# A second PSUM bank for the A3 product of a LoRA pair in a dense mixture of experts on eight cores

## The chip, the cores and the metric

The kernel runs on the 8 cores of one Trainium2 chip, two dies of four cores. Every core works on one batch element of 2048 tokens by 1024 features and has its own copy of all weights; the cores exchange nothing. The time is that of the slowest core, in microseconds (us) of the device. The engines are called PE (TensorE matmuls), PEld (TensorE weight loads), DVE (VectorE), ACT (ScalarE), POOL (GpSimd) and SP (SyncE).

## What is computed

One transformer layer: a conditionally routed attention, then a feed-forward part in which all 8 experts run on all tokens and are mixed by gates (two gates per token are not zero). The change lies in the second part. Cut to what matters:

```python
def _lora_in(xf, W, b, A, B):
    base = einsum('td,ehd->teh', xf, W)
    low = einsum('ter,ehr->teh', einsum('td,erd->ter', xf, A), B)   # r = 16
    return base + low + b
h1 = _lora_in(xf, W1, b1, A1, B1)
h3 = _lora_in(xf, W3, b3, A3, B3)
g = silu(h1) * h3
y_e = _lora_out(g, W2, b2, A2, B2)
y = einsum('te,ted->td', gates, y_e)
```

Here xf is the layer-normed input (2048 tokens per core, 1024 features), the hidden size is 2048, and the rank of A and B is 16.

## The kernel before

The kernel is written with a queue of instructions for each engine. `P.do(engine, emit, waits, inc)` appends an instruction (or a chain of matmuls) to the queue of one engine; `waits` are pairs of a semaphore and the count that it must have reached, read when the code is written, and `inc` is the semaphore that the last instruction of the entry raises. `flush` writes the queues out and leaves out a wait that the same engine has already made for the same or a higher count. Each engine works through its queue in the order written, so a wait holds back all that is behind it. `drain=True` makes the engine's next instruction wait for this one to be complete.

The stages "a" to "f" hold layer norms, routing, both attentions and the gates; they fill the first 3495 us. Stage "g", the rest, is the feed-forward part. Its outer loop `for eq_i in range(32)` runs over 8 experts (e) times 4 quarters of the hidden size (q). Weights of the next step are fetched by POOL's DMA queue into the other of two buffers (`wdma`); the small `a1te`, `a3te`, `b2te`, `b1ce`, `b3ce` have one buffer and are fetched once per expert, when the expert before has been finished. Inside it, `for tc in range(4)` runs over four blocks of 512 tokens. One pass of this inner loop puts on PE, in this order:

- only with q = 0: `mku(a1te)`, 8 matmuls that accumulate A1 times x into PSUM tile `pMISC[0:16, 0:512]` (line 1413), which DVE copies to `u1sb` (line 1426); then `mku(a3te)`, 8 matmuls of A3 times x into the same `pMISC[0:16, 0:512]`, which DVE copies to `u3sb` (line 1431). The second chain waits for the first copy. So the u products of an expert are made once for each token block, 32 times in the whole kernel.
- the gate row spread over 128 partitions, one matmul into `pch(3)` (line 1435), copied by DVE to `gateb` (line 1441).
- four times (hc), 8 + 1 matmuls for h1 into bank 0 or 2 of `pSIM` and 8 + 1 for h3 into bank 1 or 3 (lines 1452 and 1457; the ninth adds the LoRA part from `u1sb` or `u3sb`). ACT takes h1 out with Silu into `gtmp1` (line 1467) and h3 with a bias into `gtmp2` (line 1476), and DVE forms gTq from them and the gate (lines 1481 and 1487).
- 8 chains of 4 matmuls for y (line 1526; with q = 3 a fifth, line 1532, and for the first expert a sixth, line 1537), each added by DVE to `x1` (line 1549).
- `emit_u2`, 4 matmuls into `pMISC[32:48]` (line 1494), added by DVE to `u2sb` (line 1505); with q = 3 this comes ahead of the y chains.

PSUM here: `pSIM` has 2048 float32 columns per partition, four banks of 512 that `pch(0)` to `pch(3)` name; `pMISC` has one such bank. `S["mm"]` and `S["sim"]` are raised by PE, `S["vec"]`, `S["vec2"]`, `S["vec3"]`, `S["tev"]` and `S["oe"]` by DVE, `S["scl"]` and `S["scl2"]` by ACT.

Of the kernel before, what the change touches and what calls it, by code (L numbers as in the profile page):

```python
# [189 lines left out]
def build(debug_taps=()):  # L190
# [164 lines left out]
    a1te = sat("a1te", [128, 128], BF16, WS + 6400)  # L355
    a3te = sat("a3te", [128, 128], BF16, WS + 6656)
# [10 lines left out]
    pSIM = nc.alloc_psum_tensor("pSIM", [128, 2048], F32)  # L367
    pT = nc.alloc_psum_tensor("pT", [128, 2048], BF16)
    pOUT = nc.alloc_psum_tensor("pOUT", [128, 128], F32)
    pMISC = nc.alloc_psum_tensor("pMISC", [128, 512], F32)  # L370
# [10 lines left out]
    S = {k: Sem(nc, k) for k in names}  # L381
    nc.const_aps.register(F32, 1e-5, fconst[0:1, 0:1])
    P = Prog(nc, S)
# [30 lines left out]
    for _e in ("tensor", "vector", "scalar", "gpsimd"):  # L414
        P.do(_e, lambda E: E.nop(),
             waits=[(S["sdc"], SD_CONST), (S["sgc"], S["sgc"].n)])
# [41 lines left out]
    for dc in range(8):  # L458
# [3 lines left out]
             waits=ld + [(S["mm"], S["mm"].n)], inc=S["scl"], drain=True)  # L462
        def mk(d=dc):
            def f(E):
# [12 lines left out]
             inc=S["mm"])  # L477
# [5 lines left out]
    for dc in range(8):  # L483
# [3 lines left out]
             waits=ld + [(S["scl"], S["scl"].n),  # L487
                         (S["mm"], max(0, S["mm"].n - 1))],
             inc=S["vec"], drain=True)
        P.do("vector", (lambda d=dc: lambda E:  # L490
                        E.tensor_mul(xlch(d)[:, :], xlch(d)[:, :], rB[:, :]))(),
             inc=S["vec"], drain=True)
        P.do("scalar", (lambda d=dc: lambda E:
                        E.activation(xsq[:, :], xlch(d)[:, :], AF.Square))(),
             waits=[(S["vec"], S["vec"].n), (S["mm"], S["mm"].n)],
             inc=S["scl"], drain=True)
        def mk(d=dc):
# [19 lines left out]
         waits=[(S["mm"], S["mm"].n)], inc=S["vec"], drain=True)  # L517
    P.do("vector", lambda E: E.tensor_scalar_mul(c0_row, pSIM[0:1, 0:2048], 1 / 1024.0),
         inc=S["vec"], drain=True)
    P.do("vector", lambda E: E.tensor_copy(sr_row, pSIM[32:33, 0:2048]),  # L520
         inc=S["vec"], drain=True)
    P.do("vector", lambda E: E.tensor_mul(c1_row, c0_row, c0_row),
         inc=S["vec"], drain=True)
# [4 lines left out]
         waits=[(S["vec"], S["vec"].n)], inc=S["scl"], drain=True)  # L528
    P.do("scalar", lambda E: E.activation(sr_row, sr_row, AF.Sqrt),
         inc=S["scl"], drain=True)  # L530
    P.do("vector", lambda E: E.reciprocal(c1_row, t_row),
         waits=[(S["scl"], S["scl"].n)], inc=S["vec"], drain=True)
    P.do("vector", lambda E: E.tensor_scalar_max(sr_row, sr_row, 1e-12),
         inc=S["vec"], drain=True)
    P.do("vector", lambda E: E.reciprocal(sr_row, sr_row), inc=S["vec"], drain=True)
    P.do("vector", lambda E: E.tensor_scalar_mul(sr_row, sr_row, 32.0),
         inc=S["vec"], drain=True)
    P.do("vector", lambda E: E.tensor_mul(c0_row, c0_row, c1_row),
         inc=S["vec"], drain=True)
    P.do("vector", lambda E: E.tensor_scalar_mul(c0_row, c0_row, -1.0),  # L540
         inc=S["vec"], drain=True)
# [3 lines left out]
    if "route_s" in debug_taps:  # L545
# [5 lines left out]
         waits=[(S["vec"], S["vec"].n)], inc=S["c1p"], drain=True)  # L551
    cur_eps = 4.0
    logk = math.log(1152.0)
    for it in range(20):
        inv = 1.0 / cur_eps
        P.do("gpsimd", lambda E: E.tensor_sub(u_rt, s_rt, rl_rt),
             waits=[(S["c1s"], S["c1s"].n), (S["c1p"], S["c1p"].n)],
             inc=S["c1p"], drain=True)
        P.do("vector", lambda E: E.reduce_max(sc_rt[:, 0:1], u_rt, axis=AX.X),
             waits=[(S["c1p"], S["c1p"].n)], inc=S["c1v"], drain=True)  # L560
# [3 lines left out]
             inc=S["c1v"], drain=True)  # L564
# [3 lines left out]
             waits=[(S["c1v"], S["c1v"].n)], inc=S["c1s"], drain=True)  # L568
        P.do("vector", lambda E: E.reduce_sum(sc_rt[:, 2:3], rl_rt, axis=AX.X),
             waits=[(S["c1s"], S["c1s"].n)], inc=S["c1v"], drain=True)  # L570
        P.do("scalar", lambda E: E.activation(sc_rt[:, 3:4], sc_rt[:, 2:3], AF.Ln),
             waits=[(S["c1v"], S["c1v"].n)], inc=S["c1s"], drain=True)
        P.do("gpsimd", lambda E: E.tensor_sub(sc_rt[:, 4:5], sc_rt[:, 3:4],
                                              sc_rt[:, 1:2]),
             waits=[(S["c1s"], S["c1s"].n)], inc=S["c1p"], drain=True)
# [3 lines left out]
             inc=S["c1p"], drain=True)  # L579
        P.do("scalar", lambda E: E.activation(rl_rt, s_rt, AF.Relu,  # L580
                                              bias=sc_rt[:, 5:6], scale=1.0),
             waits=[(S["c1p"], S["c1p"].n)], inc=S["c1s"], drain=True)
# [5 lines left out]
    for dc in range(8):  # L588
# [3 lines left out]
             waits=ld + [(S["scl"], S["scl"].n)], inc=S["vec"], drain=True)  # L592
        P.do("vector", lambda E: E.tensor_mul(xlt[:, :], xlt[:, :], rB[:, :]),
             inc=S["vec"], drain=True)
        P.do("vector", lambda E: E.tensor_mul(xlt[:, :], xlt[:, :], c1B[:, :]),
             inc=S["vec"], drain=True)
        P.do("vector", lambda E: E.tensor_add(xlt[:, :], xlt[:, :], c0B[:, :]),
             inc=S["vec"], drain=True)
# [4 lines left out]
             inc=S["vec"], drain=True)  # L603
    P.flush("p2b")
    if "ln2T" in debug_taps:
# [4 lines left out]
          inc=S["sgw"])  # L610
# [788 lines left out]
    for eq_i in range(32):  # L1399
# [4 lines left out]
        if q == 0:  # L1404
            P.do("vector", lambda E: E.memset(u2sb, 0.0),
                 waits=[(S["mm2"], S["mm2"].n)], inc=S["vec3"], drain=True)
        for tc in range(4):
            if q == 0:
                def mku(att, tc=tc):
                    def f(E):  # L1410
                        ins = None
                        for dc in range(8):
                            ins = E.matmul(pMISC[0:16, 0:512],  # L1413
                                           att[:, 16 * dc:16 * dc + 16],
                                           xl2T[:, 2048 * dc + 512 * tc:
                                                2048 * dc + 512 * tc + 512],
                                           start=(dc == 0), stop=(dc == 7))
                        return ins
                    return f
                P.do("tensor", mku(a1te),  # L1420
                     waits=[sg_at[eq_i], (S["scl2"], S["scl2"].n),
                            (S["vec3"], S["vec3"].n), (S["vec"], S["vec"].n),
                            (S["sim"], S["sim"].n)],
                     inc=S["mm"])
                P.do("vector", (lambda tc=tc: lambda E:
                                E.tensor_copy(u1sb[:, 512 * tc:512 * tc + 512],
                                              pMISC[0:16, 0:512]))(),
                     waits=[(S["mm"], S["mm"].n)], inc=S["vec"], drain=True)
                P.do("tensor", mku(a3te), waits=[(S["vec"], S["vec"].n)], inc=S["mm"])
                P.do("vector", (lambda tc=tc: lambda E:  # L1430
                                E.tensor_copy(u3sb[:, 512 * tc:512 * tc + 512],  # L1431
                                              pMISC[0:16, 0:512]))(),
                     waits=[(S["mm"], S["mm"].n)], inc=S["vec"], drain=True)
            P.do("tensor", (lambda e=e, tc=tc: lambda E:
                            E.matmul(pch(3), sel8[:, 128 * e:128 * e + 128],  # L1435
                                     gatesF[:, 512 * tc:512 * tc + 512],
# [161 lines left out]
```

How the kernel before makes its waits and increments, by code:

```python
                    def body(E):  # L169
                        seen = {}
                        prev_pend = [None]
                        for (waits, emit, inch, k, pend) in ops:
                            allw = list(waits)
                            if prev_pend[0] is not None:
                                allw.append(prev_pend[0])
                            for (s, n) in allw:
                                h = s.h
                                if seen.get(id(h), -1) < n:
                                    E.wait_ge(h, n)
                                    seen[id(h)] = n
                            ins = emit(E)
                            if inch is not None:
                                ins.then_inc(inch, k)
                            prev_pend[0] = (pend[0], pend[1]) if pend else None
```

## Time and profile before

| what | us |
|---|---|
| median of 2 timed runs | 7972.79 |
| the two runs | 7962.31 and 7983.27 |
| the profiled execution, its own time | 7924.43 |
| span of its slowest core (core 1) | 7922.9 |
| spans of its eight cores | 7885.8 to 7922.9 |

The profiled execution is one run of the same program, recorded by the hardware. Its span goes from the first to the last instruction of one core, and its own time adds what lies around that (1.5 us). Durations are read from this execution, which is 48.4 us, or 0.6%, below the median of the timed runs. "Busy" sums the time in which an engine worked; "granted clock" is the share of TensorE's full 2.4 GHz that was granted in a stretch, 0.50 being the lower of the two levels, 1.2 GHz.

### The profile page before, as it was taken

To read this page: it belongs to the slowest core of one execution; us is meant where nothing else is said; L and a number is where in the kernel's file an instruction comes from. 1 tells how busy PE (TensorE), PEld (TensorE's weight loads), DVE (VectorE), ACT (ScalarE), POOL (GpSimd) and SP (SyncE) were. 2 spreads that over 40 slices of the span, in tenths; PEclk is the share of its full clock that TensorE was granted. 3 is DMA by queue.
4 is the path that set the end of the run, shared out by engine and by line. 5 is a ranking of instruction groups with operands and counts; after the bars stand their busy time and mean duration, and the time that the engine had idled before them with its cause. 6 is when DMAs were issued, how large, how long until landed. Compare 5 with 4: busy or idle time off the path is not lost.

```text
span 7922.9 us, 72055 instructions; the slowest of 8 cores (7885.8 to 7922.9 us)
## 1 busy us (share of the span) xinstructions
PE 5513.9 (70%) x22384; PEld 2099.6 (27%) x22384; DVE 3300.1 (42%) x6024; ACT 1412.4 (18%) x1824; POOL 305.9 (4%) x337
## 2 busy tenths in 40 slices
PE   5141133247687776238888889889888888898897
PEld 1020000113454452013223323223233233232232
DVE  2755444476666662443323333333233233333332
ACT  1012100002343341011111111111111111111111
POOL 0012100000000000000000000000000000000000
PEclk8575555566555557569879989999899899898998
DMA  2110000020000001021211112121212112121211
GB/s 94 52 11 0 0 0 0 6 48 6 1 1 1 1 1 53 1 33 17 33 17 20 30 17 33 17 33 17 33 17 33 17 17 33 17 33 17 33 17 43
DMA packets 149719, 169.26 MB, mean 21 GB/s; under 512 B 56132, under 2 KB 125268, under 8 KB 142948
## 3 DMA queue, kind: packets, MB, share of 16 engines
q0 software_dynamic: 140688, 111.63, 9.5%
q1 hardware_dynamic: 8660, 53.04, 1.9%
q8 instruction: 191, 3.13, 0.2%
q14 instruction: 180, 1.47, 0.1%
HBM read 267.68 MB, written 8.39 MB: 35 GB/s over the span
## 4 chain that ended last, share of the span: by engine, by line
PE 47%; DVE 5%; issue 3%; ACT 1%; DMA 1%; POOL 0%; DVEq 0%; ACTq 0%; PEldq 0%; POOLq 0%
PE pSIM L1452 24%; PE pSIM L1526 13%; PE pSIM L1457 4%; DVE x L1549 2%; PE pMISC L1413 2%; PE pMISC L1494 2%; PE pSIM L1532 1%; ACT gtmp L1476 1%; DVE gTq L1487 1%; DVE gtmp L1481 1%; DMA b3ce<-b3c 1%; DVE u2sb L1505 0%; PE pSIM L1435 0%; DVEq L179 0%; DVE u3sb L1431 0%
## 5 line engine op out<-in xcount | busy, mean ns | idle before, releaser
L1526 PE MATMUL pSIM<-gTq,w2b 128*128 128x512 bf16 x4096 | 1203.7, 441 | 310.3 <-DVE gTq L1487 225.5
L1549 DVE SCALAR_TENSOR_TENSOR x<-pSIM,x 128x512 f32<-128x512 f32 x1024 | 708.3, 692 | 780.4 <-PE pSIM L1526 445.8
L1452 PE MATMUL pSIM<-xl2T,w1b 128*128 128x512 bf16 x4096 | 997.5, 387 | 21.1 <-DVE u3sb L1431 21.1
L1481 DVE TENSOR_TENSOR gtmp<-gtmp,gtmp 128x512 bf16<-128x512 bf16 x512 | 217.7, 425 | 1870.9 <-ACT gtmp L1476 1870.9
L1452 PE MATMUL pSIM<-xl2T,w3b 128*128 128x512 bf16 x4096 | 972.9, 380 | 0.0
L1467 ACT ACTIVATE gtmp<-pSIM,b1ce 128x512 bf16<-128x512 f32 x512 | 352.8, 689 | 2950.3 <-PE pSIM L1457 2923.8
L1526 PEld LDWEIGHTS pSIM<-gTq,w2b 128*128 128x128 bf16 x4096 | 385.0, 108 | 1051.1 <-issue 862.7
L1452 PEld LDWEIGHTS pSIM<-xl2T,w1b 128*128 128x128 bf16 x4096 | 363.7, 99 | 517.6 <-issue 165.6
L1452 PEld LDWEIGHTS pSIM<-xl2T,w3b 128*128 128x128 bf16 x4096 | 358.6, 98 | 481.2 <-issue 118.4
L824 PE MATMUL pT<-idbf,lattnT 128*128 128x128 bf16 x128 | 33.9, 265 | 648.5 <-DVE lattnT L819 648.5
L1476 ACT ACTIVATE gtmp<-pSIM,b3ce 128x512 bf16<-128x512 f32 x512 | 352.6, 689 | 716.2 <-PE pSIM L1457 716.2
L1025 DVE TENSOR_REDUCE smwk<-pSIM 128x1 f32<-128x512 f32 x512 | 354.1, 692 | 59.6 <-PE pSIM L1006 6.2
L1072 PE MATMUL pOUT<-attnT,hv 128*65 128x128 bf16 x2048 | 265.8, 309 | 39.4 <-DVE attnT L1102 25.9
L1006 PE MATMUL pSIM<-hk,hq 64*128 64x512 bf16 x512 | 240.4, 620 | 10.7 <-ACT attnbf L1045 5.3
L1487 DVE TENSOR_TENSOR gTq<-gtmp,gateb 128x512 bf16<-128x512 bf16 x512 | 217.7, 425 | 55.8 <-DVE gtmp L1481 3.2
L1063 PE MATMUL pT<-idbf,attnbf 128*128 128x128 bf16 x2048 | 240.6, 312 | 0.0
L1072 PEld LDWEIGHTS pOUT<-attnT,hv 128*65 128x65 bf16 x2048 | 210.3, 169 | 84.4 <-issue 68.8
L1063 PEld LDWEIGHTS pT<-idbf,attnbf 128*128 128x128 bf16 x2048 | 206.9, 145 | 52.5 <-issue 52.3
L1057 ACT COPY attnT<-pT 128x1024 bf16<-128x1024 bf16 x128 | 129.6, 1013 | 506.0 <-PE pT L1063 506.0
L1457 PE MATMUL pSIM<-u1sb,b1tqb 16*128 16x512 bf16 x512 | 199.6, 390 | 0.0
L1129 PE MATMUL pMISC<-denrow,ones_f 1*128 1x256 f32 x128 | 76.0, 695 | 175.4 <-DVE denrow L1124 132.9
L1494 PE MATMUL pMISC<-gTq,a2tqb 128*16 128x512 bf16 x512 | 150.5, 422 | 68.3 <-DVE gTq L1487 68.3
(265 smaller groups left out, 4779.5 us busy)
## 6 DMA issues: line engine op xcount, KB each, us to landing
w1b<-w1q POOLq DMA_DIRECT2D x32, 1024.0 KB, 9.6
w3b<-w3q POOLq DMA_DIRECT2D x32, 1024.0 KB, 13.7
w2b<-w2q POOLq DMA_DIRECT2D x32, 1024.0 KB, 16.8
xs<-xT SPq DMA_DIRECT2D x24, 1024.0 KB, 4.8
xc<-xT SPq DMA_DIRECT2D x16, 1024.0 KB, 4.9
out<-x SPq DMA_DIRECT2D x8, 1024.0 KB, 10.2
wst<-wqkv POOLq DMA_DIRECT2D x8, 256.0 KB, 5.1
cos<-cos SPq DMA_DIRECT2D x1, 1024.0 KB
```

What stands on the lines that cost most here:

```text
L1025: E.reduce_max(smwk[:, 2 + kc:3 + kc], pSIM[:, 512 * kc:512 * kc + 512], axis=AX.X))(),
L1063: ins = E.transpose(pT[:, 1024 * half + 128 * (j - j0): 1024 * half + 128 * (j - j0) + 128], attnbf[:, 128 * j:128 * j + 128], idbf[:, :])
L1072: ins = E.matmul(pOUT[0:65, 0:128], hv[:, 520 * j + 65 * h:520 * j + 65 * h + 65], attnT[:, 128 * j:128 * j + 128], start=(start and j == ...
L1452: E.matmul(pSIM[:, 512 * bank:512 * bank + 512], wb[:, 512 * dc + 128 * hc:512 * dc + 128 * hc + 128], xl2T[:, 2048 * dc + 512 * tc: 2048 ...
L1457: return E.matmul(pSIM[:, 512 * bank:512 * bank + 512], btq[:, 128 * hc:128 * hc + 128], usb[:, 512 * tc:512 * tc + 512], start=False, sto ...
L1467: E.activation(gtmp1[:, :], pSIM[:, 512 * b:512 * b + 512], AF.Silu, bias=b1ce[:, hcg:hcg + 1], scale=1.0))(),
L1476: E.activation(gtmp2[:, :], pSIM[:, 512 * b:512 * b + 512], AF.Identity, bias=b3ce[:, hcg:hcg + 1], scale=1.0))(),
L1481: P.do("vector", lambda E: E.tensor_mul(gtmp1[:, :], gtmp1[:, :], gtmp2[:, :]), waits=[(S["scl"], S["scl"].n), (S["scl2"], S["scl2"].n), ( ...
L1487: E.tensor_mul(gTq[:, 512 * hc:512 * hc + 512], gtmp1[:, :], gateb[:, :]))(),
L1494: ins = E.matmul(pMISC[32:48, 0:512], a2tqb[par][:, 16 * hc:16 * hc + 16], gTq[:, 512 * hc:512 * hc + 512], start=(hc == 0), stop=(hc == 3))
L1526: ins = E.matmul(pch(yb), w2b[par][:, 1024 * hc + 128 * dc: 1024 * hc + 128 * dc + 128], gTq[:, 512 * hc:512 * hc + 512], start=(hc == 0), ...
L1549: E.scalar_tensor_tensor(x1[:, 2048 * dc + 512 * tc: 2048 * dc + 512 * tc + 512], pch(yb), 1.0, x1[:, 2048 * dc + 512 * tc: 2048 * dc + 51 ...
```

## The change

The chain for A3 now writes columns 1024 to 1535 of `pSIM`, bank 2, partitions 0 to 15, in place of `pMISC`, and DVE copies it from there. Its wait for DVE's copy of the A1 product is replaced: it waits for DVE's copy of the A3 product of the token block before (`u3ev`), and for ACT's last reads of `pSIM` (`scl`, `scl2`). The A1 chain waits for its own last copy (`u1ev`) in place of the newest count of `vec`; its other waits stay. In the first token block of an expert neither dictionary has an entry, and both chains wait for the newest count of `vec`, as before; for the A3 chain that is the copy of the A1 product.

```diff
+        if q == 0:
+            u1ev, u3ev = {}, {}
         for tc in range(4):
             if q == 0:
-                def mku(att, tc=tc):
+                def mku(att, dst, tc=tc):
                     def f(E):
                         ins = None
                         for dc in range(8):
-                            ins = E.matmul(pMISC[0:16, 0:512],
+                            ins = E.matmul(dst,
                                            att[:, 16 * dc:16 * dc + 16],
...
-                P.do("tensor", mku(a1te),
+                P.do("tensor", mku(a1te, pMISC[0:16, 0:512]),
                      waits=[sg_at[eq_i], (S["scl2"], S["scl2"].n),
-                            (S["vec3"], S["vec3"].n), (S["vec"], S["vec"].n),
+                            (S["vec3"], S["vec3"].n),
+                            (S["vec"], u1ev.get(tc - 1, S["vec"].n)),
                             (S["sim"], S["sim"].n)],
                      inc=S["mm"])
...
-                P.do("tensor", mku(a3te), waits=[(S["vec"], S["vec"].n)], inc=S["mm"])
+                u1ev[tc] = S["vec"].n
+                P.do("tensor", mku(a3te, pSIM[0:16, 1024:1536]),
+                     waits=[(S["vec"], u3ev.get(tc - 1, S["vec"].n)),
+                            (S["scl"], S["scl"].n), (S["scl2"], S["scl2"].n)],
+                     inc=S["mm"])
                 P.do("vector", (lambda tc=tc: lambda E:
                                 E.tensor_copy(u3sb[:, 512 * tc:512 * tc + 512],
-                                              pMISC[0:16, 0:512]))(),
+                                              pSIM[0:16, 1024:1536]))(),
                      waits=[(S["mm"], S["mm"].n)], inc=S["vec"], drain=True)
+                u3ev[tc] = S["vec"].n
```

No instruction is added, removed or moved on any engine; waits differ. PE's queue at the start of the second token block of an expert, with the waits that are left after `flush`, before:

```order
L1494 MATMUL pMISC<-gTq,a2tqb_155 16x512 x4
L1413 MATMUL pMISC<-xl2T,a1te 16x512 [waits vec3,sim]
L1413 MATMUL pMISC<-xl2T,a1te 16x512 x7
L1413 MATMUL pMISC<-xl2T,a3te 16x512 [waits vec]
L1413 MATMUL pMISC<-xl2T,a3te 16x512 x7
L1435 MATMUL pSIM<-gatesF,sel_56 128x512 [waits oe]
L1452 MATMUL pSIM<-xl2T,w1b_165 128x512 [waits vec]
```

The same place in PE's queue after the change (lines are numbered 2 to 8 higher there):

```order
L1502 MATMUL pMISC<-gTq,a2tqb_155 16x512 x4
L1415 MATMUL pMISC<-xl2T,a1te 16x512 [waits vec3,sim]
L1415 MATMUL pMISC<-xl2T,a1te 16x512 x7
L1415 MATMUL pSIM<-xl2T,a3te 16x512 x8
L1443 MATMUL pSIM<-gatesF,sel_56 128x512 [waits oe]
L1460 MATMUL pSIM<-xl2T,w1b_165 128x512 [waits vec]
```

The A3 chain has lost its only wait; the A1 chain keeps its waits for `vec3` and `sim`, and the first h1 matmul its wait for `vec`. This holds for token blocks 2 to 4 of each expert, 24 times. At the first token block of the kernel's first expert the queue reads, after the change:

```order
L1415 MATMUL pMISC<-xl2T,a1te 16x512 [waits sgp0,scl2,vec3,vec,sim]
L1415 MATMUL pMISC<-xl2T,a1te 16x512 x7
L1415 MATMUL pSIM<-xl2T,a3te 16x512 [waits vec,scl]
L1415 MATMUL pSIM<-xl2T,a3te 16x512 x7
L1443 MATMUL pSIM<-gatesF,sel_56 128x512 [waits tev,vec2,oe]
```

There the A3 chain still waits for `vec`, and so it does at the first block of the seven other experts.

## Rows read from the trace of the kernel before

**Rows 1.** The page: its head, and busy time by engine.
```profile
span 7922.9 us, 72055 instructions; the slowest of 8 cores (7885.8 to 7922.9 us)
PE 5513.9 (70%) x22384; PEld 2099.6 (27%) x22384; DVE 3300.1 (42%) x6024; ACT 1412.4 (18%) x1824; POOL 305.9 (4%) x337
```

**Rows 2.** Windows: stretch, busy us of PE, PEld, DVE, ACT, POOL; granted clock; DMA.
```profile
0.00:3450.00 3450.00, 1647.32 (x7632) 779.04 (x7632) 1902.15 (x3606) 701.94 (x793) 140.03 (x105) 0.57 0.06 16
3495.00:7922.00 4427.00, 3866.53 (x14752) 1320.56 (x14752) 1388.78 (x2407) 706.70 (x1025) 153.81 (x215) 0.91 0.15 25
```

**Rows 3.** Waits of PE, 3495 to 7922 us: total us, times, longest.
```profile
PE pSIM L1526 <- DVE gTq L1487: 225.5, 96, 2.7
PE pMISC L1413 <- DMA b3ce<-b3c: 129.5, 8, 88.7
...
PE pMISC L1413 <- DVE u1sb L1426: 32.0, 32, 1.0
PE pMISC L1413 <- DVE u2sb L1505: 26.7, 24, 1.1
...
PE pSIM L1452 <- DVE u3sb L1431: 21.1, 32, 0.7
```

**Rows 4.** Timeline at the first expert's fourth token block: start, duration, what.
```profile
3607.61 0.68 DVE L1505 SCALAR_TENSOR_TENSOR u2sb<-pMISC,u2sb 16x512 f32<-16x512 f32 x1 [0.27 <-PE pMISC L1494]
...
3608.54 1.89 PE L1413 MATMUL pMISC<-xl2T,a1te 128*16 128x512 bf16 x8 [1.11 <-DVE u2sb L1505]
3610.60 0.68 DVE L1426 CAST u1sb<-pMISC 16x512 bf16<-16x512 f32 x1 [2.31 <-PE pMISC L1413]
...
3611.43 1.89 PE L1413 MATMUL pMISC<-xl2T,a3te 128*16 128x512 bf16 x8 [1.00 <-DVE u1sb L1426]
...
3613.25 0.39 PE L1435 MATMUL pSIM<-gatesF,sel 8*128 8x512 bf16 x1
3613.49 0.68 DVE L1431 CAST u3sb<-pMISC 16x512 bf16<-16x512 f32 x1 [2.21 <-PE pMISC L1413]
3614.27 0.69 DVE L1441 CAST gateb<-pSIM 128x512 bf16<-128x512 f32 x1
...
3614.32 0.59 PE L1452 MATMUL pSIM<-xl2T,w1b 128*128 128x512 bf16 x2 [0.68 <-DVE u3sb L1431]
```

**Rows 5.** The chain that ended last, the second expert's second token block.
```profile
4120.50 1.90 PE pMISC L1413 x8
...
4122.57 0.69 DVE u1sb L1426
...
4123.39 1.90 PE pMISC L1413 x8
...
4125.45 0.69 DVE u3sb L1431
...
4126.28 1.89 PE pSIM L1452 x8
```

**Rows 6.** Timeline: the A3 chains of token blocks 2 to 4, first and last of 24.
```profile
3538.82 1.89 PE L1413 MATMUL pMISC<-xl2T,a3te 128*16 128x512 bf16 x8 [1.00 <-DVE u1sb L1426]
...
7473.78 1.89 PE L1413 MATMUL pMISC<-xl2T,a3te 128*16 128x512 bf16 x8 [1.00 <-DVE u1sb L1426]
```

**Rows 7.** Timeline: both chains of the fourth expert's first token block.
```profile
5171.19 3.57 PE L1413 MATMUL pMISC<-xl2T,a1te 128*16 128x512 bf16 x8 [5.97 <-DMA b3ce<-b3c]
...
5175.77 3.57 PE L1413 MATMUL pMISC<-xl2T,a3te 128*16 128x512 bf16 x8 [1.00 <-DVE u1sb L1426]
```

**Rows 8.** Windows, columns as in rows 2: 10 us of h chains; three passes.
```profile
3510.00:3520.00 10.00, 10.00 (x43) 3.66 (x42) 1.70 (x4) 3.97 (x6) 0.00 (x0) 1.00 0.01 2
5216.43:5251.86 35.43, 29.85 (x127) 10.65 (x126) 11.67 (x20) 5.51 (x8) 0.00 (x0) 1.00 0.00 0
5251.86:5289.18 37.32, 31.69 (x127) 11.23 (x126) 11.67 (x20) 5.51 (x8) 0.00 (x0) 0.95 0.00 1
6271.50:6311.60 40.10, 34.54 (x127) 11.85 (x126) 11.67 (x20) 5.51 (x8) 0.00 (x0) 0.86 0.27 46
```

**Rows 9.** Cores: two of the eight, span and mean granted clock.
```profile
core 0: 7885.8 us, clock 0.767
core 1: 7922.9 us, clock 0.763
```

## The prediction

> **What bounds the kernel now.** I read the page first, for who is busy. PE is busy for 5513.9 of 7922.9 us [rows 1]. The windows then show two unlike halves: up to 3450 us PE works 1647 us at a mean granted clock of 0.57, from 3495 us on it works 3867 of 4427 us at 0.91 [rows 2]. The second half is the expert stage, in which the change lies, and there PE is the bound: DVE has work for 1389 of the same 4427 us, less than a third. What can be won in this stage is therefore idle time of PE and time at the lower clock, and nothing in the first 3495 us is touched.
>
> The list of waits, for that stage, says where PE stands still [rows 3]. The largest is the wait of the first y chain for gTq, 225.5 us in 96 pieces. The 129.5 us for a DMA are mostly the fetch ahead of the stage (88.7 us in one piece); the other seven come to 40.8 us, 5.8 us each, at the start of an expert. The A3 chain waits for the copy of the A1 product 32 times, 32.0 us together, 1.00 us each. Two waits stand on either side of it: the A1 chain for the sum into u2sb (24 times, 26.7 us), and the first h1 chain for the copy of u3 (32 times, 21.1 us). The change can touch the middle one alone.
>
> The timeline of one such place shows it in order [rows 4]: PE starts the A1 chain at 3608.54, DVE's copy runs from 3610.60 for 0.68 us, the A3 chain starts at 3611.43. Then the gate matmul follows at 3613.25 with no gap, DVE copies u3 from 3613.49, and h1 starts at 3614.32 after 0.68 us of waiting. The chain of waits that ended last runs through this place: chain, copy, chain, copy, chain [rows 5]. So a microsecond taken out between the two chains moves everything behind it forward.
>
> **What the change removes.** In token blocks 2 to 4 of each expert, 3 x 8 = 24 times, the A3 chain has no wait left and goes behind the A1 chain at once. In the first token block of each expert it still waits for the A1 copy, so 8 of the 32 waits stay at 1.00 us. The price of one removed wait can be read as a distance between starts, which includes the end of the pipeline. From the A1 chain to the A3 chain it is 3611.43 - 3608.54 = 2.89 us. What it will be without the wait has its nearest row in the next step: from the A3 chain to the gate matmul, which follows without a wait, it is 3613.25 - 3611.43 = 1.82 us. The gain is 2.89 - 1.82 = 1.07 us a time, and 24 x 1.07 = 25.7 us. The lower end is the idle time as shown, 24 x 1.00 = 24.0 us. For the upper end the A3 chain would follow with the spacing that matmuls have inside a chain. A chain of 8 is recorded with 1.89 us and one matmul alone with 0.39 [rows 4], so seven spacings take 1.50 us, 0.214 each, and eight 1.71. The upper end is 24 x (2.89 - 1.71) = 28.3 us. I take 25.7, whose row has a chain of the same 8 matmuls in front.
>
> The Trainium skill, "TensorE: Matmul & The Clock Gate", section "Back-to-back issue gap", puts the spacing at the full clock at columns / 2.4 GHz plus about 2.5 ns, 216 ns for 512 columns. By that rule the chain would be followed after 1.73 us and the sum would be 24 x 1.16 = 27.8 us, an estimate near my upper end; the rows show 1.82 us at a change of the weights' shape, and the choice between the two is worth 2 us.
>
> All 24 places run at the full clock, as the first and the last of them show: 1.89 us for a chain of 8 [rows 6], against 3.57 us at 1.2 GHz where an expert has just waited for its DMA [rows 7]. The eight places at the lower clock are first blocks, where the wait stays. So no part of the 24 is worth more because PE is slow there.
>
> **What the change moves or adds.** DVE's copy of u1, 0.68 us, now lies beside the A3 chain of 1.89 us; it is done about 1 us before that chain ends, and DVE is idle then (it waited 2.21 us for the A3 chain [rows 4]). The cover therefore holds. What is late next is the u3 copy, 0.68 us between the A3 chain and h1, as now: the wait of 21.1 us in 32 pieces stays and is not larger. It is 0.68 us since the gate matmul covers part of the copy, and that matmul stays in its place. If DVE were late with u1 by over 1 us it would be late with u3 as well, and h1 would wait for it; nothing in rows 4 makes it late.
>
> The added waits cost nothing. PE's wait for `scl` and `scl2` asks for ACT's last reads of pSIM in the token block before; the y chains have already waited for the same counts, so in blocks 2 to 4 no wait is written. The wait for the u3 copy of the block before was passed by the h1 chains. In the first block of the kernel `scl` is asked for, 88.7 us of DMA wait [rows 3] behind ACT's last work of the stage before. The A1 chain's weaker wait for `vec` wins nothing either, since the y chains waited for a later count; what holds it is u2sb, 1.11 us [rows 4], which stays. Bank 2 is next written by the second h1 chain, over 5 us after the copy of u3 began, and h1 has waited for that copy. No DMA is moved: the weights wait for the ends of steps, each about 3 us earlier after a q = 0 step, and the DMA engines are used to 0.15 [rows 2].
>
> **The clock.** A pass has a second part that the change can shift without touching it. Of the 24 passes from a gate matmul to the next that contain one of the changed places, most show the granted clock falling once, at the first y chains, behind the wait for gTq (225.5 / 96 = 2.3 us each [rows 3]); such a pass takes 37.32 us at 0.95. Three are under 36 us, and the best of them has 1.00 and 35.43 us; one has 0.86 and 40.10 us [rows 8]. So one fall costs about 1.9 us, and whether it comes differs between passes that do the same work. The cores differ in the same way, 7885.8 against 7922.9 us with the same program, the slower at a slightly lower clock [rows 9]. Moving each pass by 1.07 us can turn falls on or off here and in the later quarters. I take zero for the mean of that, and allow for it in the range: 10 falls more or fewer are 19 us.
>
> **The sum.** On the profiled execution: 7924.4 - 25.7 = 7898.7 us. The median of the timed runs stands 48.4 us higher, with 10.5 us to either side between its two runs; most of that difference I cannot assign to any place, so I carry it over: 7972.8 - 25.7 = 7947.1 us, rounded to 7947. That is 0.3% less, far inside the 2% (159 us) that a measurement of this kernel can tell from no change.
>
> **The rivals.**
>
> 1. The clock gives more. For it: most changed passes carry a fall worth 1.9 us, and an idle microsecond less per pass is activity gained. If the 21 passes with a fall lost it, 21 x 1.9 = 40 us would come on top: 7972.8 - 25.7 - 39.9 = 7907 us. Against it: the falls come behind the wait for gTq, 20 us away from the place changed.
>
> 2. The wait only moves. The A3 chain would start at once, but PE would be held as long somewhere else, by the u3 copy ahead of h1 or by the y chains' wait for gTq. For it: the next wait is one step away. Against it: each of these is measured from a PE event that comes 1.07 us earlier too, and DVE is idle in between. It gives 7973 us. The same time comes out if the waits in `flush` did not fall away, but PE's queue shows them gone.
>
> 3. Slower: the clock takes it back. The place is the first y chains of the same 24 passes, where a pass of 40.10 us at 0.86 exists beside those of 37.32 at 0.95 [rows 8], so a second stretch at 1.2 GHz is possible there and costs 2.8 us. If the new timing brought it to all 24, the cost would be 24 x 2.78 - 25.7 = +41 us, 8014 us. It decides from 25.7 / 2.78, that is 10 such passes of 24, on. For it: the timing of the falls shifts with every pass. Against it: one pass of 24 has it now, and no PE idle time is added anywhere.
>
> Beside this rival stands a rule that speaks against alternating banks: the Trainium skill, "TensorE: Matmul & The Clock Gate", section "A second HAM failure mode: psum-queue depth-cycling", says that a kernel whose matmul groups cycled through PSUM banks idled briefly between groups so often that the clock went up and down. By that rule the u chains, now in two banks, would start such falls. The trace speaks against it in this kernel: the h chains change the bank with every nine matmuls, and 10 us of them show PE busy for 10.00 us at a granted clock of 1.00 [rows 8]. If the rule held, the time would be that of rival 3.
>
> **How the numbers follow.** The waits go and the clock's share stays small: 0.65. Rival 1: 0.10. Rival 2: 0.12. Rival 3, taken to begin where the gain is used up: 0.11. Anything that no row shows, 0.02. The predicted time is 7947. The two timed runs scatter by 10.5 us around their median, the terms of the sum by 2, the clock by 19: the likeliest case alone spans 7920 to 7975. To hold 8 in 10 I reach down to rival 1's time and up past rival 2 and the near part of rival 3: 7908 to 7988. For a change over 2% the whole gain would have to be six times as large, or the clock rival nearly four times what 24 passes can give: faster 0.01, within 2% 0.98, slower 0.01.
>
> **What would show it.** In the profile after the change: the wait of the A3 chain for u1sb falls from 32 times and 32.0 us to 8 times and 8.0 us. The start of an A3 chain in blocks 2 to 4 lies 1.7 to 1.85 us behind the A1 chain's. h1's wait for u3sb stays at 32 times and about 21 us, the A1 chain's for u2sb at 24 and 26.7. A pass without a clock fall takes 34.4 us in place of 35.43. The prediction is wrong in its first step if the A3 chain still waits or if the spacing stays near 2.9 us, in its second if the wait for u3sb or gTq grows by what was removed, and in its third if the granted clock of the expert stage leaves 0.91 by more than 0.01 (1% of 4427 us is more than the whole gain).

## The result and the profile after

The changed kernel is faster by 0.8%: the ratio of its time to that of the kernel before is 0.9922, with a 95% interval of 0.9900 to 0.9945. Put on the 7972.79 us of before that is 7911 us (7893 to 7929), 44 to 80 us less. The median over all 13 of its runs, 8000.59 us, is no measure of the change, since seven of them fell into a disturbed state in which one die or both ran at a lower clock; the ratio leaves those out. The forecast was 7947 us, a gain of 25.7 us, in a range of 7908 to 7988; the 7911 us lie 3 us inside its lower end.

The profiled execution took 7898.8 us, 25.6 us less than the profiled one of before. That this is the forecast term to 0.1 us is chance, as the stages will show. Its page begins:

```profile
span 7897.3 us, 71715 instructions; the slowest of 8 cores (7859.5 to 7897.3 us)
PE 5462.1 (69%) x22069; PEld 2098.8 (27%) x22384; DVE 3299.4 (42%) x6024; ACT 1409.0 (18%) x1824; POOL 305.9 (4%) x337
```

315 of the 22384 matmul records are missing in this core's trace, so its PE busy time is not compared with [rows 1]. PE's waits in the expert stage (slowest core, core 2, 3455 to 7900 us; total, times, longest) answer to [rows 3]:

```profile
PE pSIM L1534 <- DVE gTq L1495: 224.9, 96, 2.7
PE pMISC L1415 <- DMA b3ce<-b3c: 137.4, 8, 85.7
...
PE pMISC L1415 <- DVE u2sb L1513: 26.7, 24, 1.1
...
PE pSIM L1460 <- DVE u3sb L1438: 25.0, 32, 0.9
...
PE pSIM L1415 <- DVE u1sb L1429: 8.1, 8, 1.1
```

The wait for u1sb went from 32 times and 32.0 us to 8 times and 8.1 us. Its neighbours are as before: u2sb 26.7, gTq 224.9 against 225.5, and u3sb 25.0 against 21.1 us (20.6 on core 1). Nothing took its place. The timeline at the second expert's second block, core 1, answers to [rows 4]:

```profile
4134.18 1.89 PE L1415 MATMUL pMISC<-xl2T,a1te 128*16 128x512 bf16 x8 [1.11 <-DVE u2sb L1513]
4135.90 1.89 PE L1415 MATMUL pSIM<-xl2T,a3te 128*16 128x512 bf16 x8
4136.24 0.68 DVE L1429 CAST u1sb<-pMISC 16x512 bf16<-16x512 f32 x1 [2.31 <-PE pMISC L1415]
4137.73 0.38 PE L1443 MATMUL pSIM<-gatesF,sel 8*128 8x512 bf16 x1
```

The A3 chain starts 1.72 us behind the A1 chain, where it was 2.89; the copy of u1 lies beside it. The windows of the same core show what the forecast had no term for. First the stretch of q = 0 of the first and second expert and the sum over all eight experts, of the kernel before (length, then busy PE, PEld, DVE, ACT, POOL, granted clock, DMA):

```profile
3503.49:3644.71 141.22, 120.75 (x485) 42.75 (x485) 45.62 (x79) 23.33 (x33) 0.00 (x0) 0.96 0.02 3
4088.07:4228.90 140.83, 120.55 (x486) 42.86 (x485) 45.62 (x79) 22.05 (x32) 0.00 (x0) 0.96 0.10 16
...
sum 1136.46, PE 973.70 PEld 344.56 DVE 364.89 ACT 177.62 POOL 0.00; mean PE 121.71 PEld 43.07 DVE 45.61 ACT 22.20 POOL 0.00
```

The same of the changed kernel:

```profile
3518.06:3652.71 134.65, 117.13 (x485) 42.03 (x485) 45.62 (x79) 23.32 (x33) 0.00 (x0) 0.98 0.02 3
4101.73:4236.35 134.62, 116.97 (x486) 42.16 (x485) 45.63 (x79) 22.04 (x32) 0.00 (x0) 0.98 0.08 14
...
sum 1084.28, PE 942.80 PEld 338.45 DVE 364.91 ACT 177.61 POOL 0.00; mean PE 117.85 PEld 42.31 DVE 45.61 ACT 22.20 POOL 0.00
```

On this core q = 0 is 52.2 us shorter, twice the forecast term, and PE was busy for 31 us less with the same matmuls: they ran at the higher clock more often, 0.98 against 0.96. One pass of each, the second expert's, before and then after:

```profile
4125.21:4162.01 36.80, 31.37 (x126) 11.17 (x126) 11.68 (x20) 5.51 (x8) 0.00 (x0) 0.95 0.00 0
```

```profile
4137.73:4172.00 34.27, 29.69 (x127) 10.72 (x126) 11.68 (x20) 5.51 (x8) 0.00 (x0) 1.00 0.00 0
```

36.80 to 34.27 us is 2.53, of which the wait is 1.16. The rest, 1.37 us, is a fall of the clock that is no longer there: before, the first 16 y matmuls behind the wait for gTq took 5.30 us, now the first 8 take 1.89.

I counted this for all eight cores, from the starts of the gate matmuls and the granted clock. "With a fall" is a pass from one gate matmul to the next with over 1 us below the full clock (at 1.2 GHz in all but one of the passes counted in the table). "Block 2" is the pass that starts at the gate matmul of token block 2 and holds the u chains of block 3; "block 3" is the next one, with the u chains of block 4. There are 64 of each, 8 experts on 8 cores. "Typical" is the median of those without any fall. The third changed place of an expert, the u chains of block 2, lies in the pass from the gate matmul of block 1. That pass had a fall in all 64 cases of both kernels, so a third of the changed passes gained nothing from the clock.

| kernel | passes with a fall, block 2 / block 3 | typical pass without a fall, block 2 | q = 0, mean of 8 cores |
|---|---|---|---|
| before | 84% / 78% | 35.43 us | 1131.5 us |
| changed | 22% / 23% | 34.27 us | 1091.4 us |

A block 2 pass with a fall takes 36.81 us before and 35.64 after (medians). So q = 0 lost 40.1 us on the average core. The two terms make that up: 24 x 1.16 = 27.8 us for the waits, and 104 passes with a fall less 29, over 8 cores, is 9.4 falls a core, times 1.38 = 12.9 us.

The average hides one thing. Two cores of the changed kernel's execution, 2 and 3, ran the fifth expert's q = 0 in 151.5 and 147.8 us, where the other six took 134.3 to 137.1. For 92 and 95 us of it they were granted a third level of the clock, 0.81, which the trace of before does not have at all. Core 2:

```profile
5704.90:5856.40 151.50, 133.51 (x475) 45.60 (x485) 45.59 (x79) 21.99 (x32) 0.00 (x0) 0.84 0.08 13
```

On the other six cores q = 0 took 1088.1 us, against 1131.3 us on the same six before, 43.2 us less. The two terms, 40.7 us, leave 2 to 3 us of that unassigned. In the quarters q = 2 and q = 3 the mean core was 3.3 and 3.8 us slower than before, so that from the first gate matmul to the last the profiled execution gained 33.3 us.

### The profile page after: what moved, and what is told of

The parts are those of the page before. It is cut to its first block, busy times and chain, and to the rows that moved or that the text cites. A ratio compares the mean times of both kernels' runs of the same rounds, so it can differ in the third digit from the quotient of the medians.

```text
span 7897.3 us, 71715 instructions; the slowest of 8 cores (7859.5 to 7897.3 us)
## 1 busy us (share of the span) xinstructions
PE 5462.1 (69%) x22069; PEld 2098.8 (27%) x22384; DVE 3299.4 (42%) x6024; ACT 1409.0 (18%) x1824; POOL 305.9 (4%) x337
## 4 chain that ended last, share of the span: by engine, by line
PE 46%; DVE 5%; issue 3%; ACT 1%; DMA 1%; POOL 0%; DVEq 0%; another core or an unknown queue 0%; ACTq 0%; PEldq 0%; POOLq 0%
PE pSIM L1460 24%; PE pSIM L1534 12%; PE pSIM L1465 4%; DVE x L1557 2%; PE pMISC L1502 2%; PE pSIM L1540 1%; ACT gtmp L1484 1%; PE pMISC L1415 1%; PE pSIM L1415 1%; DVE gtmp L1489 1%; DVE gTq L1495 1%; DMA b3ce<-b3c 1%; DVE u2sb L1513 0%; PE pSIM L1443 0%; DVEq L179 0%
## 5 line engine op out<-in xcount | busy, mean ns | idle before, releaser
L1534 PE MATMUL pSIM<-gTq,w2b 128*128 128x512 bf16 x4001 | 1178.4, 438 | 324.3 <-DVE gTq L1495 224.9
L1460 PE MATMUL pSIM<-xl2T,w1b 128*128 128x512 bf16 x3984 | 978.8, 387 | 31.4 <-DVE u3sb L1438 25.0
L1063 PEld LDWEIGHTS pT<-idbf,attnbf 128*128 128x128 bf16 x2048 | 207.0, 145 | 52.4 <-issue 52.2
L1465 PE MATMUL pSIM<-u3sb,b3tqb 16*128 16x512 bf16 x512 | 198.2, 387 | 1.3
```

The source lines that it names most:

```text
L1063: ins = E.transpose(pT[:, 1024 * half + 128 * (j - j0): 1024 * half + 128 * (j - j0) + 128], attnbf[:, 128 * j:128 * j + 128], idbf[:, :])
L1460: E.matmul(pSIM[:, 512 * bank:512 * bank + 512], wb[:, 512 * dc + 128 * hc:512 * dc + 128 * hc + 128], xl2T[:, 2048 * dc + 512 * tc: 2048 ...
L1465: return E.matmul(pSIM[:, 512 * bank:512 * bank + 512], btq[:, 128 * hc:128 * hc + 128], usb[:, 512 * tc:512 * tc + 512], start=False, sto ...
L1534: ins = E.matmul(pch(yb), w2b[par][:, 1024 * hc + 128 * dc: 1024 * hc + 128 * dc + 128], gTq[:, 512 * hc:512 * hc + 512], start=(hc == 0), ...
```

## Experiments

**The theories.** The wait is gone and is worth 1.16 us each. Open was why the falls went. Theory timing: whether the clock falls behind the 2.3 us wait for gTq depends on when that wait comes, counted from the falls or waits before, and the change moved it. Theory activity: PE has one idle microsecond less per pass, so the clock holds. Beside them stands the question whether bank 2 does anything of its own.

**The bank without the wait's removal.**

```diff
-                     waits=[(S["vec"], u3ev.get(tc - 1, S["vec"].n)),
+                     waits=[(S["vec"], S["vec"].n),
```

> The A3 chain writes bank 2 of pSIM as in the change, but still waits for DVE's copy of the A1 product in all 32 places. Every theory in which the removed wait does the work expects the kernel before: 32 waits of 1.00 us, a ratio of 1.000, and in token blocks 2 and 3 of q = 0 the passes of 36.8 us with a fall of the clock in about 8 of 10. A theory in which the bank itself matters expects part of the gain, a ratio near 0.995.

The ratio was 1.0002 (0.9963 to 1.0041), and the wait was back in full (core 1, PE's waits):

```profile
PE pSIM L1415 <- DVE u1sb L1429: 32.1, 32, 1.1
```

No gain of the bank by itself shows, and the interval rules out one of 0.4% or more. What the bank does is to give the A3 product a place of its own, so that the wait can go. In its profiled execution, 92% and 70% of the passes had time below the full clock; part of that was at 0.81, and 89% and 61% had a fall to 1.2 GHz (84% and 78% before).

**The wait's removal without the other bank.** The A3 product stays in pMISC, in another group of 32 partitions.

```diff
-                P.do("tensor", mku(a3te, pSIM[0:16, 1024:1536]),
-                     waits=[(S["vec"], u3ev.get(tc - 1, S["vec"].n)),
-                            (S["scl"], S["scl"].n), (S["scl2"], S["scl2"].n)],
+                P.do("tensor", mku(a3te, pMISC[64:80, 0:512]),
+                     waits=[(S["vec"], u3ev.get(tc - 1, S["vec"].n))],
```

> The wait is removed as in the change, but the A3 product stays in pMISC, at partitions 64 to 79. If only the wait matters: the changed kernel again, 8 waits left, passes of 34.3 us, a ratio of 0.992 to 0.995. If a write to the bank that DVE reads costs time, the spacing of the two chains exceeds 1.75 us or the copy exceeds 0.68 us.

The ratio was 0.9933 (0.9910 to 0.9956), as expected, but the typical pass took 33.42 us and not 34.3, 0.85 us less than in the changed kernel. The timeline of core 1 tells why:

```profile
4101.79 1.24 PE L1415 MATMUL pMISC<-xl2T,a1te 128*16 128x512 bf16 x5 [1.11 <-DVE u2sb L1512]
4102.65 0.38 PE L1415 MATMUL pMISC<-xl2T,a3te 128*16 128x512 bf16 x1
4102.86 0.38 PE L1415 MATMUL pMISC<-xl2T,a1te 128*16 128x512 bf16 x1
4102.88 0.38 PE L1415 MATMUL pMISC<-xl2T,a3te 128*16 128x512 bf16 x1
...
4103.31 1.24 PE L1415 MATMUL pMISC<-xl2T,a3te 128*16 128x512 bf16 x5
...
4104.48 0.39 PE L1442 MATMUL pSIM<-gatesF,sel 8*128 8x512 bf16 x1
```

The A3 chain starts 0.86 us behind the A1 chain's start, and from there A1 and A3 matmuls start in pairs, 0.01 to 0.02 us apart. Two matmuls whose outputs lie in different groups of 32 partitions ran at the same time. The Trainium skill, "TensorEngine Tiling (Array Packing)", section "Key Properties", says that tiles of the array work independently and can load weights and multiply in parallel; these rows agree, for outputs of 16 partitions and a full contraction of 128. Falls: 38% and 62%.

**Work in place of the wait.** These kernels put matmuls that nobody reads between the two chains of blocks 2 to 4. The first sent them to free partitions:

```diff
+                if tc > 0:
+                    def fill(tc=tc):
...
+                            for dc in range(5):
+                                ins = E.matmul(pMISC[64:80, 0:512],
+                                               a1te[:, 16 * (dc % 8):16 * (dc % 8) + 16],
+                                               xl2T[:, 512 * tc:512 * tc + 512],
+                                               start=True, stop=True)
```

> The changed kernel with 5 further matmuls of 512 columns, 1.07 us of work that is used for nothing, between the A1 and the A3 chain of token blocks 2 to 4 of q = 0. The passes have the timing of the kernel before, but PE works where it stood still. Theory timing (whether the clock falls behind the wait for gTq depends on when in time that wait comes): the falls are back in about 8 of 10 passes of blocks 2 and 3, these take 36.8 us, and the ratio is 0.999 to 1.000. Theory activity (the falls went since PE has one idle microsecond less): falls stay at 2 to 3 of 10, the passes take 35.4 us, and the ratio is about 0.997.

This one did not test what it was meant to. The five matmuls ran beside the A1 chain and took no time: the typical pass stayed at 34.27 us, falls at 17% and 22%, the ratio 0.9952 (0.9926 to 0.9978). It is in effect a second copy of the changed kernel, and so a measure of how far such ratios scatter.

With 15 of them some stick out (`range(15)`):

> As with 5 further matmuls, but 15 of them, 3.2 us of work, so that a pass is 0.7 us longer than a pass with a fall in the kernel before. Theory timing: the share of passes with a fall changes once more against the 5 matmuls, and can be as low as in the changed kernel, 37.5 us a pass. Theory activity: 2 to 3 of 10 with a fall, as with 5 matmuls. Without falls the sum is 24 x 3.2 = 77 us over the changed kernel, a ratio near 1.002; with a fall in 8 of 10 passes it is 25 us more.

Passes without a fall took 35.80 us, since about 8 of the 15 hid beside the A1 chain; falls came in 84% and 86%; the ratio was 1.0031 (1.0002 to 1.0060). Theory activity had 2 to 3 of 10, and PE has no more idle time here than in the changed kernel (17.5 us in the first expert's q = 0 on core 1 in both, 20.5 before), so this already speaks against it. Theory timing had only said that the share would change. Its hint that a pass of 37.5 us could have few falls was not tested, since the pass was not as long as planned.

The clean form sends five to the output partitions that the two chains use:

```diff
-                                ins = E.matmul(pMISC[64:80, 0:512],
+                                ins = E.matmul(pSIM[0:16, 1024:1536],
...
-                    P.do("tensor", fill())
+                    P.do("tensor", fill(),
+                         waits=[(S["vec"], u3ev[tc - 1]),
+                                (S["scl"], S["scl"].n), (S["scl2"], S["scl2"].n)])
```

> The 5 further matmuls of token blocks 2 to 4 now go to pSIM bank 2, partitions 0 to 15, the same output partitions as the A1 and A3 chains, since the ones sent to partitions 64 to 79 ran beside the A1 chain and took no time. Here they are to take 5 x 0.215 = 1.07 us, so that a pass without a fall has 35.3 us as in the kernel before, but with PE busy in place of idle. Theory timing: falls in about 8 of 10 passes of blocks 2 and 3, the typical pass 36.8 us, ratio 0.998 to 1.001. Theory activity: falls in 2 to 3 of 10, the typical pass 35.3 us, ratio about 0.996.

The timeline shows the place filled, with no idle time of PE from the A1 chain to the gate matmul:

```profile
4119.15 1.67 PE L1415 MATMUL pMISC<-xl2T,a1te 128*16 128x512 bf16 x7
4120.65 1.24 PE L1438 MATMUL pSIM<-xl2T,a1te 128*16 128x512 bf16 x5
...
4121.73 1.89 PE L1415 MATMUL pSIM<-xl2T,a3te 128*16 128x512 bf16 x8
4123.56 0.38 PE L1457 MATMUL pSIM<-gatesF,sel 8*128 8x512 bf16 x1
```

The window of the pass behind it (core 1, second expert) has the clock fall again:

```profile
4123.56:4160.28 36.72, 32.29 (x131) 11.72 (x131) 11.68 (x20) 5.50 (x8) 0.00 (x0) 0.95 0.00 0
```

Falls came in 78% and 69% of the passes (84 and 78 before, 22 and 23 changed), the typical pass without one took 35.35 us, q = 0 took 1127.9 us on the mean core, and the ratio was 0.9994 (0.9947 to 1.0041). PE does more work here than in the changed kernel and has no idle microsecond there, and the falls are back. The ratio alone would not decide, since its interval holds both theories' values, but the falls do: theory activity is out.

Timing fits, and the order of the falls supports it. In each of these kernels the passes of blocks 2 and 3 have the same work and differ by at most 0.35 us in their typical length, yet whether it has a fall goes with the pass before it. In the changed kernel, 48 of the 50 experts (counted per core) without a fall in the block 2 pass had none in the block 3 pass, and 13 of the 14 with one had one again. In the kernel of the next experiment, the A1/A3 pair, it is the opposite: none of 28 had a fall twice running, and 31 of the 36 without one had one in the next pass. With the A3 product in pMISC it alternates as well: 20 of 24 falls were followed by none, and 36 of 40 passes without one by a fall. How the chip arrives at that was not taken apart.

**A and B chains in pairs.** One matmul of A1 and one of A3 in turn, in two partition groups of pMISC, both copies behind them; no wait between the chains in any of the 32 places.

```diff
+                            E.matmul(pMISC[0:16, 0:512],
+                                     a1te[:, 16 * dc:16 * dc + 16], xs_,
+                                     start=(dc == 0), stop=(dc == 7))
+                            ins = E.matmul(pMISC[64:80, 0:512],
+                                           a3te[:, 16 * dc:16 * dc + 16], xs_,
+                                           start=(dc == 0), stop=(dc == 7))
```

> A1 and A3 matmuls alternate, one to pMISC partitions 0 to 15 and one to 64 to 79; DVE copies both behind the pair, in all 32 places. Theory overlap (two matmuls to different groups of 32 output partitions run at once): the 16 matmuls take 1.9 us in place of 3.6, from the first of them to h1 it is about 3.6 us in place of 5.8 before, a pass without a fall has about 33.2 us, and in the 8 places at 1.2 GHz 4 to 5 us go. Ratio 0.985 to 0.990. Without overlap: 16 matmuls take 3.5 us, h1 follows after 5.3 us, and the ratio is 0.996 to 0.999.

The ratio was 0.9897 (0.9876 to 0.9918) and the typical pass 33.34 us. The sixteen matmuls run from 4098.25 to 4100.15, 1.90 us:

```profile
4098.25 0.38 PE L1415 MATMUL pMISC<-xl2T,a1te 128*16 128x512 bf16 x1 [1.11 <-DVE u2sb L1507]
4098.25 0.38 PE L1418 MATMUL pMISC<-xl2T,a3te 128*16 128x512 bf16 x1
...
4099.76 0.38 PE L1415 MATMUL pMISC<-xl2T,a1te 128*16 128x512 bf16 x1
4099.77 0.38 PE L1418 MATMUL pMISC<-xl2T,a3te 128*16 128x512 bf16 x1
4100.08 0.39 PE L1437 MATMUL pSIM<-gatesF,sel 8*128 8x512 bf16 x1
```

The overlap is shown. Falls came in 44% and 48%, another share at another length of the pass. The ratio rests on two runs of this kernel.

The pair with one more copy by DVE ahead of its two was meant as the opposite of the busy variant, more idle time at the changed kernel's length of pass:

```diff
+                for _ in range(1):
+                    P.do("vector", (lambda tc=tc: lambda E:
+                                    E.tensor_copy(u1sb[:, 512 * tc:512 * tc + 512],
+                                                  pMISC[0:16, 0:512]))(),
+                         waits=[(S["mm"], S["mm"].n)], inc=S["vec"], drain=True)
```

> The pair with one more copy by DVE (A1 product to u1sb, 0.78 us with its wait) ahead of the two: more PE idle time per pass than in the kernel before, while the pass without a fall has 34.0 us, close to the changed kernel. Theory timing: falls in few passes of blocks 2 and 3, 2 to 4 of 10. Theory activity: falls in 8 of 10 or more. Ratio 0.988 to 0.994.

It missed both theories. The ratio was 1.0015 (0.9979 to 1.0051), outside what both expected. Passes without a fall took 34.12 us. Passes with one were rarer than before, 58% and 42%, against activity's 8 of 10, but timing had 2 to 4 of 10, from the 22% and 23% at nearly the same length, 34.27 us. So the length of the pass alone does not fix the share. A pass with a fall took 37.3 to 37.5 us since it had two: in 63 of the 64 such passes the clock fell once 3 to 4.3 us behind the gate matmul, that is behind the longer wait ahead of h1, and once more behind the wait for gTq.

**The eight waits that were left.** The changed kernel with no wait for the A1 copy in first blocks either.

```diff
-                     waits=[(S["vec"], u3ev.get(tc - 1, S["vec"].n)),
+                     waits=[(S["vec"], u3ev.get(tc - 1, 0)),
```

> The changed kernel, in which the A3 chain also does not wait for the A1 copy in the 8 first token blocks, so that all 32 waits are gone. The 8 places run at 1.2 GHz behind the DMA wait, where the distance of the two chains was 4.57 us and is to be 3.42: 8 x 1.15 = 9 us less than the changed kernel in the stage, ratio 0.991. If the timing of the falls shifts with the first block, the falls in blocks 2 and 3 change from 2 of 10, and the 9 us are lost or doubled; if the overlap of PE work with the clock's recovery eats it (the low clock lasts as long whatever PE does), it is worth less than 9 us.

Its runs gave no ratio. In the profiled execution the stage from the first to the last gate matmul took 4293.2 us on the mean core, against 4319.9 of the changed kernel, 27 us less where 9 were expected. The timeline of a first block (core 1) shows one part of the reason:

```profile
4070.54 3.57 PE L1415 MATMUL pMISC<-xl2T,a1te 128*16 128x512 bf16 x8 [7.52 <-DMA b3ce<-b3c]
...
4073.91 2.45 PE L1415 MATMUL pSIM<-xl2T,a3te 128*16 128x512 bf16 x8
```

The A3 chain, at 3.5 to 3.6 us in six of the eight such places of core 1 before [rows 7], is back at the full clock after its first matmuls. And the pass from the first block's gate matmul, which had a fall in all 64 cases in both kernels, has one in 28%. In blocks 2 and 3, falls came in 38% and 28%, somewhat more than the changed kernel's 22% and 23%. The direction is clear; the size rests on one profile of each kernel, and without cores 2 and 3, which stood at 0.81 for a while in the changed kernel's, the stage is 4291.8 against 4313.7 us, 22 us less.

**A version that beats both.** The A1/A3 pair of the next token block goes between the h chains and the y chains, where PE waits for gTq, and its two copies behind the last gTq on DVE.

```diff
             GTC = S["vec"].n
+            if q == 0 and tc < 3:
+                emit_u13(tc + 1, False)
```

> The A1/A3 pair of the next token block is issued between the h chains and the y chains of this one (blocks 2 to 4 of each expert), where PE waits 2.3 us for gTq; the two copies go behind the last gTq on DVE. If overlap and free place both hold, the pair costs PE nothing: the q = 0 passes of blocks 1 to 3 shrink from 36.8 to 30.3 to 31 us like those of q = 1, 24 x 6 = 144 us, and 8 first blocks give 4 us each: ratio 0.975 to 0.982. If the pair does not fit into the wait, the y chains start late by 1 to 2 us and the ratio is 0.982 to 0.987.

Its median was 7745.67 us. Its set of runs gave no ratio; against the 7931.77 us of before in the set of runs ahead, that is a ratio of 0.977. In blocks 2 and 3 none of the 64 passes each had a fall, and the typical one took 29.02 us: the place was filled, and the fall behind it went with it.

The last step adds second buffers for `a1te`, `a3te`, `b1ce` and `b3ce`, loads them a step earlier, and issues the pair of an expert's first block in the last pass of the expert before.

```diff
+            if q == 3 and tc == 3 and e < 7:
+                emit_u13(0, False, e + 1)
```

> In addition a1te, a3te, b1ce and b3ce get a second buffer and are fetched one step earlier, and the pair of the next expert's first block is issued in the last pass of the expert before. The 7 waits for the DMA of 5.8 us go, and with them the stretch at 1.2 GHz behind each: 7 x (5.8 + 3.4 + 2) = 78 us on top, ratio 0.965 to 0.973. If a fall of the clock stays at that place without the DMA wait, only 7 x 8 = 56 us.

Its median was 7652.57 us, by the same 7931.77 us a ratio of 0.965. It was run again beside the kernel before:

> The same kernel as the one with early pairs and second buffers for the small weights, run again since no undisturbed run of the kernel before stood beside it: ratio 0.963 to 0.968, from 7652.6 us against the 7931.8 us that the kernel before had in the run of experiments ahead of it.

The ratio was 0.9648 (0.9605 to 0.9692), as expected. PE's waits on core 1 (3480 to 7600 us):

```profile
PE pSIM L1536 <- DVE gTq L1493: 180.5, 96, 2.5
PE pMISC L1414 <- DMA b3ce<-b3c: 78.9, 1, 78.9
```

Seven of the eight waits for the DMA are gone, and the wait for gTq fell by 45 us against [rows 3]. Its passes of q = 0 stay at the full clock (core 1, second expert, second block):

```profile
4066.74:4095.77 29.03, 27.91 (x126) 10.06 (x126) 11.68 (x20) 5.50 (x8) 0.00 (x0) 1.00 0.00 1
```

## Why the prediction was right or wrong

**The waits: right, a little small.** Eight waits of 1.0 us are left, 24 are gone, the waits for u2sb, u3sb and gTq did not grow, and u1's copy lies beside the A3 chain. Rival 2, that the wait only moves, fell. The term was 25.7 us and measured 24 x 1.16 = 27.8. The step that was off is the choice of the row for the new distance of the two chains: 1.82 us, from the A3 chain to the gate matmul, where 1.72 came true. The upper end of the term, worked out from the spacing inside a chain (1.71), was the right row; the gate matmul, which differs in shape, comes 1.82 us behind the start of a chain. The Trainium skill, "TensorE: Matmul & The Clock Gate", section "Back-to-back issue gap", has the formula by which the prediction estimated 1.73 us, and the 1.72 us agree. That section gives it for a single matmul and puts a sustained stream of 512 columns at about 131 ns each, which these rows do not show: they have 0.215 us.

**The clock: wrong.** The step "I take zero for the mean of that" failed. The granted clock in q = 0 went from 0.96 to 0.98 on core 1, and 9.4 falls a core went away, 12.9 us. The reason behind the zero was that a shift turns falls on as often as off. But the passes are no random sample: 84% of those from block 2 had a fall before and 22% after, whether one falls goes with the pass before it, and 14 of the 29 falls that were left lie in one expert, the third, on seven of the eight cores. The sign that was set for this step, the granted clock of the whole expert stage leaving 0.91 by more than 0.01, did not go off: it is 0.91 on core 2 and 0.92 on core 1. It was too coarse to see a term of 13 us in 4400. Rival 1 had the direction, and its 7907 us is inside the measured interval, but not its working: it let all 21 falls of a core go, where 9.4 a core went (75 of the 104 in blocks 2 and 3, none of the 64 behind block 1), and priced one at 1.9 us, from a block 3 pass (37.32) against a block 2 pass (35.43). Like against like it is 36.81 - 35.43 = 1.38 us. Its reason, activity gained, is refuted by the variant with five matmuls in place of the wait.

**The range.** That the 7911 us lie in it is owed to its lower end, which was drawn to rival 1's time, and not to the sum: the whole interval of the timed gain, 44 to 80 us, lies above the forecast 25.7 us and above the 28.3 us of its upper end.

**Rival 3** fell for this change: no second fall came to the passes. As a mechanism it is real: with the additional copy, passes with two falls gave the gain back. With 15 matmuls the gain was lost to single falls and longer passes. The rule of the Trainium skill, "TensorE: Matmul & The Clock Gate", section "A second HAM failure mode: psum-queue depth-cycling", that was set beside it does not show here: with the bank changed and the wait kept, the ratio is 1.0002.

**The sum.** Waits and clock together give 40.7 us, and the profiled q = 0 shows 40.1, or 43.2 without the two cores that were granted 0.81. The timed gain is 44 to 80 us. The copy by accident, with five hidden matmuls, has the same passes and a gain of 0.2% to 0.7%, 17 to 59 us; both intervals hold 44 to 59 us. The shortest run of the changed kernel, 7880.91 us, is 49 us below the shortest of the kernel before in its own set of runs (7929.96) and 38 to 44 us below the shortest in the three later sets (7918.56 to 7924.81). Some 40 to 45 us are thus well supported; whether there are more, as the upper part of the interval would allow, stays open. That the two profiled executions differ by only 25.6 us came from 40 us gained in q = 0 and some 14 us given back elsewhere, where both kernels do the same work: 5.4 us ahead of the first gate matmul and 7.1 in q = 2 and q = 3 on the mean core.

## What to carry to other kernels

Price a removed wait by the distance of starts, with matmuls of the same shape for what it will be. Then count the falls of the clock in the passes around it, and do not let them average out: identical passes repeat or alternate an outcome, so a shift of 1 us can change most of them at once (84% to 22% here). A gap of PE behind which the clock falls is worth filling with independent work, which takes the gap and the fall (36.8 to 29.0 us a pass here), rather than being moved about. Two small chains, here with 16 outputs each, belong side by side, matmul by matmul, in different groups of 32 partitions.

## What was not expected

- Two matmuls of 128 x 16 weights and 512 columns, one to partitions 0 to 15 and one to 64 to 79 of the same bank, start within 0.01 us of each other, and 16 of them take 1.90 us, what 8 take alone (1.89).
- How often a 2.3 us wait of PE is followed by a fall of the clock changes with the length of the pass: 84% and 78% at 35.43 us, 78% and 69% at 35.35 us, 84% and 86% at 35.80 us, 22% and 23% at 34.27 us, 38% and 62% at 33.42 us, in blocks 2 and 3. Length is not all: with the additional copy it was 58% and 42% at 34.12 us.
- In the profiled execution of the changed kernel, cores 0 to 3 were granted 0.81 of the clock for 143 to 176 us each, cores 0 and 1 at nearly the same times and cores 2 and 3 at others; in that of the kernel before, no core was.
- The removed wait in a first block, behind a DMA wait at the lower clock, came with about 3 us less a place instead of 1.1, by one profile, the falls of the passes behind it included.
